# Where the value products and the side tasks stand in TensorE's attention slots

## The reference

```python
# x: (8, 512, 128); 16 heads of 8 features; everything float32
mod = (silu(c) @ wmod).reshape(8, 6, 1, 128)      # sa, ca, ga, sb, cb, gb
h = layernorm(x) * (1 + ca) + sa
q, k, v = split(h @ w_qkv)                         # to heads (8, 16, 512, 8)
attn = softmax(q @ k.T / sqrt(128))
x = x + ga * (merge(attn @ v) @ w_out)
h = layernorm(x) * (1 + cb) + sb
scores = softmax(h @ w_router)                     # 8 experts, the top 2, renormalised
y = sum_e comb[:, e] * ((silu(h @ w_gate[e]) * (h @ w_up[e])) @ w_down[e])
x = x + gb * y
```

## Time and profile before

| | us |
|---|---|
| median of 3 runs | 687.15 |
| span of the profiled execution | 679.4 |
| what lies around it, against the median | 7.75 |
| PE busy | 618.9 (91%) |
| DVE busy | 550.1 (81%) |
| ACT busy | 450.5 (66%) |
| POOL busy | 267.2 (39%) |

### The profile page before, as it was taken

How to read it: one execution, slowest core, us unless ns; L and a number is a source line. 1 busy time by engine, 2 the same in 40 slices (tenths; PEclk the granted TensorE clock), 3 DMA queues, 4 the chain that set the end, 5 groups by cost and what they waited for, 6 DMA issues and landing times.

```text
span 679.4 us, 13009 instructions
## 1 busy us (share of the span) xinstructions
PE 618.9 (91%) x3413; PEld 285.7 (42%) x3413; DVE 550.1 (81%) x1065; ACT 450.5 (66%) x859; POOL 267.2 (39%) x384
## 2 busy tenths in 40 slices
PE   5299999999999999999999999889899999999995
PEld 3112223323323322322322322225667777777773
DVE  3698889899888988988988988714788888888885
ACT  2107878778778778778778777876554555555553
POOL 4522022222222222222122122333567776776773
PEclk9658999999999999999999999979899999999999
DMA  7703505304304304303403400253334454345411
GB/s 183 197 31 82 183 3 117 106 20 106 117 19 95 126 17 95 127 17 79 143 18 72 150 18 4 76 167 109 92 114 139 137 142 141 130 137 150 136 35 31
DMA packets 48972, 65.58 MB, mean 97 GB/s; under 512 B 9432, under 2 KB 30432, under 8 KB 48928
## 3 DMA queue, kind: packets, MB, share of 16 engines
q1 hardware_dynamic: 46304, 64.32, 33.1%
q10 hardware_dynamic: 2624, 0.79, 0.5%
HBM read 47.26 MB, written 17.83 MB: 96 GB/s over the span
## 4 chain that ended last, share of the span: by engine, by line
PE 34%; DVE 20%; issue 19%; POOL 16%; ACT 5%; DMA 2%; SPq 1%; DVEq 1%; POOLq 0%; ACTq 0%
POOL hid_lo L612 13%; DVE negmax L864 13%; PE o_acc L1172 11%; PE s_row L1149 10%; PE s_col L1162 5%; ACT probs L656 3%; DVE probs L1042 1%; POOL h_lo L618 1%; PE misc L1130 1%; PE misc L1103 1%; PE misc L1100 1%; SPq L325 1%; DVE sums_inv L883 1%; DVE k_rest L878 1%; PE misc L1126 1%
## 5 line engine op out<-in xcount | busy, mean ns | idle before, releaser
L864 DVE TENSOR_REDUCE negmax<-s_row 128x1 f32<-128x512 f32 x512 | 323.0, 683 | 47.5 <-PE s_row L1149 41.9
L656 ACT ACTIVATE probs<-s_col 128x512 f32<-128x512 f32 x512 | 270.8, 599 | 76.4 <-PE s_col L1162 73.4
L1149 PE MATMUL s_row<-k_stack,q_stack 64*128 64x512 bf16 x512 | 141.7, 402 | 25.2 <-DMA k_stack<-k_scr 11.6
L612 POOL TENSOR_TENSOR hid_lo<-probs,hid_hi 128x512 fp32r<-128x512 f32 x87 | 128.5, 1493 | 61.9 <-ACT hid_hi L800 61.9
L1162 PE MATMUL s_col<-q_stack,k_stack 64*128 64x512 bf16 x512 | 132.4, 383 | 7.1 <-ACT probs L656 6.5
L1172 PE MATMUL o_acc<-probs,v_aug 128*32 128x512 f32 x1024 | 138.1, 612 | 0.0
L800 ACT ACTIVATE hid_hi<-probs 128x512 fp32r<-128x512 f32 x88 | 55.6, 632 | 85.0 <-DVE probs L1042 84.6
L1149 PEld LDWEIGHTS s_row<-k_stack,q_stack 64*128 64x128 bf16 x512 | 34.9, 93 | 180.1 <-DVE negmax L864 142.1
L1042 DVE TENSOR_TENSOR probs<-probs,q_stack 128x512 f32<-128x512 f32 x56 | 62.5, 1116 | 15.7 <-POOL hid_lo L612 13.6
L520 POOL CAST negmax_parts<-negmax 128x16 bf16<-128x16 f32 x32 | 6.3, 196 | 163.0 <-DVE negmax L864 163.0
L1032 DVE TENSOR_TENSOR probs<-probs,s_col 128x512 f32<-128x512 f32 x88 | 59.6, 677 | 2.9 <-ACT probs L820 1.6
(11 more groups left out here) (134 smaller groups left out, 713.9 us busy)
## 6 DMA issues: line engine op xcount, KB each, us to landing
q_scr<-q_parts SPq DMA_DIRECT2D x48, 128.0 KB, 2.4
k_scr<-k_parts SPq DMA_DIRECT2D x48, 128.0 KB, 2.4
q_stack<-q_scr SPq DMA_DIRECT2D x8, 768.0 KB, 6.1
k_stack<-k_scr SPq DMA_DIRECT2D x8, 768.0 KB, 7.5
q_stack<-combT_scr SPq DMA_DIRECT2D x24, 256.0 KB, 3.4
k_stack<-combT_scr SPq DMA_DIRECT2D x16, 224.0 KB, 2.9
q_stack<-combT_scr SPq DMA_DIRECT2D x16, 192.0 KB, 2.7
q_stack<-combT_scr SPq DMA_DIRECT2D x16, 160.0 KB, 2.6
```

Of the source, the lines that this page charges most:

```text
L612: nc.gpsimd.tensor_tensor(hid_lo[k % HIDDEN][:], weighed[(par + k) % 2], hid_hi[k % HIDDEN][:], ALU.subtract).then_inc(s["hid_split"], 1)
L656: nc.scalar.activation(probs[t % 2][:, j, :], s_col[score_bank("col", u)][:], ACT.Exp, scale=INV_SCALE).then_inc(s["exp_done"], 1)
L864: nc.vector.tensor_reduce(negmax[n % 2][:, j, qc:qc + 1], s_row[score_bank("row", u)][:], AX.X, ALU.max, negate=True).then_inc(s["row_max" ...
L1149: nc.tensor.matmul(s_row[score_bank("row", u)][:], q_stack[par][at:at + KS, head // 2, P * qc:P * (qc + 1)], k_stack[par][at:at + KS, head ...
```

## The change

The order on PE in a slot becomes R0 R1 C0 C1, R2 R3, W, C2 C3, task, task. No task stands at place 0 any more: both remaining places are at the end of the slot. The table TASKS is written anew for it, and with it the places at which ACT makes the middle parts of q and k, and DVE the remainders of q and k, the layer norm's statistics (two per place) and the router's steps. No instruction is added or taken away. The changed file has 20 lines less at its head, so line numbers are lower by 20.

```diff
     TASKS = {
-        (0, 0): "xT", (0, 2): "max1", (1, 0): "q", (2, 0): "k", (3, 0): "o0", (3, 2): "o1", (4, 0): "o2", (4, 2): "max2",
-        (5, 0): "o3", (5, 1): "attnT", (6, 0): "proj", (8, 1): "max3", (9, 0): "v", (10, 2): "x1T", (11, 1): "router",
-        (12, 1): "max0", (15, 0): "combT",
+        (0, 1): "xT", (0, 2): "max1", (1, 2): "q", (2, 2): "k", (3, 1): "o0", (3, 2): "o1", (4, 1): "o2", (4, 2): "max2",
+        (5, 1): "o3", (6, 1): "attnT", (7, 1): "proj", (8, 2): "max3", (9, 2): "v", (10, 2): "x1T", (11, 2): "router",
+        (12, 1): "max0", (15, 2): "combT",
     }
...
-            MIDDLE_Q, MIDDLE_K, ROUTER_EXP, FIRST_BLOCK = (2, 0), (3, 0), (12, 0), (14, 1)
+            MIDDLE_Q, MIDDLE_K, ROUTER_EXP, FIRST_BLOCK = (2, 1), (3, 1), (12, 1), (14, 1)
...
-            REST = {(1, 2): "q", (2, 2): "k"}
-            LN2_STATS = [(6, 1), (7, 0), (7, 1), (8, 0), (8, 1)]
-            ROUTE = {(12, 1): softmax_sum, (13, 0): sort, (13, 1): pick, (14, 0): denominator}
+            REST = {(2, 0): "q", (3, 0): "k"}
+            LN2_STATS = {(8, 0): (0, 1), (8, 1): (2, 3), (9, 0): (4,)}
+            ROUTE = {(12, 2): softmax_sum, (13, 1): sort, (14, 0): pick, (14, 1): denominator}
...
                 for t in range(SLOTS):
-                    def scores(j):
-                        if t < SLOTS - AHEAD:
-                            row_scores(b, par, t + AHEAD, j)
-                        elif not last:
-                            row_scores(b + 1, 1 - par, t + AHEAD - SLOTS, j)
                     for half in range(2):
                         for j in range(2 * half, 2 * half + 2):
-                            scores(j)
+                            if t < SLOTS - AHEAD:
+                                row_scores(b, par, t + AHEAD, j)
+                            elif not last:
+                                row_scores(b + 1, 1 - par, t + AHEAD - SLOTS, j)
+                        if half == 1 and t > 0:
+                            weigh(b, par, t - 1)
+                        elif half == 1 and not first:
+                            weigh(b - 1, 1 - par, SLOTS - 1)
+                        for j in range(2 * half, 2 * half + 2):
                             col_scores(b, par, t, j)
-                        turn((t, half))
-                    if t > 0:
-                        weigh(b, par, t - 1)
-                    elif not first:
-                        weigh(b - 1, 1 - par, SLOTS - 1)
+                    turn((t, 1))
                     turn((t, 2))
```

More of the change, by code:

```diff
@@ L993, in body @@
                         if not first:
-                            if at in LN2_STATS:
-                                ln2_stats(b - 1, LN2_STATS.index(at))
+                            for step in LN2_STATS.get(at, ()):
+                                ln2_stats(b - 1, step)
                             if at in ROUTE:
```

## The result

The changed kernel takes 785.35 us, the median of four runs (783.63 to 787.21), against 687.21 (686.04 to 687.64, four runs) for the kernel before beside it: 1.145 times as long (95% interval 1.140 to 1.151). Slower, as forecast, but by 98 us and not by 53. In experiments 2, 4 and 6 one of the four runs was in a slower state of the chip: it counts in the median and in the span of times given there, and not in the ratio.

The account below looks back on a forecast made before the run. PE's chain, with PE and DVE waiting for each other, was taken as the bound. Span 679.4 + 49 (six batches) + 1.5 (batch 0) + 2 (batch 7) = 732, plus 7.75 around it: 740 us; range 706 to 760.

Parts of the forecast that it names:

- The order on PE without a task: PE's slot without a task: the new order takes 2.72 us against 2.71, so the order alone is worth nothing.
- The tasks on the chain: All tasks stand between C3 and R0, uncovered on PE's chain: their products add 11.7 us a batch.
- The second task's wait: End of slots 0, 3, 4: max1 waits 1.3 us for ACT, o1 and max2 0.7 each for DVE.
- The failed step: SP's transfers for next q and k start some 4 us later, slot 8 some 6 us later: costs nothing.
- If that cover is gone, R0 of slot 8 waits a few us a batch: Proviso on SP's loads of the next q and k: uncovered, slot 8's first row product waits a few us a batch.
- The clock: Rival: PE's standstill in slot 0 halves its clock, 3 us a batch, +25, about 765 us; chance 0.10.
- ACT's and DVE's side work: ACT's moved middle parts of q and k cost nothing; DVE's extra work before maxima an estimated 1.4 us a batch.
- Batch 0: First batch, without output tasks: about 49.5 us against 47.79, +1.5.
- Batch 7: Last batch: +4 in slots 0 to 7, -2 from slot 8; together +2, give or take 4.
- What lies around the span: Time outside the profiled span: 7.75 us between span and median, taken as unchanged and added to 732.
- DVE became the bound: Rival: maxima never wait, so DVE sets the batch at 46.0 us; 651 us, weaker form 660; chance 0.10.
- Tasks bare: Rival: tasks uncovered on PE but the waits of max1 and o1 hidden, 700 to 728 us; chance 0.18.

Follow-up runs that it names:

- experiment 2: Changed kernel with the old order on PE, its task tables kept as changed: 745.84 us, ratio 1.089 to the kernel before.
- experiment 4: Changed kernel with DVE's sum of the router's exponents moved from the end of slot 12 to the middle of slot 13: 783.74 us, ratio 1.143.
- experiment 6: Changed kernel in which SP waits for max2's store before loading the next batch's q and k: 759.27 us, ratio 1.108.
- experiment 1: Kernel before with only the new order on PE, all its tasks where they were: 711.30 us, ratio 1.040.
- experiment 3: Changed kernel with ACT's placing of max2 at the head of slot 7 instead of slot 6: 765.42 us, ratio 1.117.
- experiment 5: Experiment 3 with max1, o1 and max2 moved to place 0 of the slot that follows: 732.33 us, ratio 1.066.
- experiment 9: Experiment 6 with five extra copies of the coming R0 on PE between xT and max1 in slot 0: 759.28 us, ratio 1.110.
- experiment 8: Kernel before, old PE order, with attnT, x1T, router moved to place 0, proj to slot 7, and max2's placing to slot 7: 672.03 us, ratio 0.982.

## Why the forecast held in sign and not in size

**The order on PE without a task: right.** 2.72 was worked out, 2.70 measured, with C1 at 0.85 (0.84) and no wait of the value products. That this makes the order worth nothing holds without a task only (experiment 1).

**The tasks on the chain: right.** Slots 2, 5, 8 to 12, 14 and 15, each with one task or none, came out within 0.1. DVE's wait for row products rose to 82.3 where "70 or more" was forecast, but that sign was met by luck: without the late store it is 67.0 (experiment 3) and 65.6 (experiment 6), just under it.

**The second task's wait: right.** max1 1.44 (1.3), o1 0.68 and max2 0.87 (0.7 each). Experiment 5 takes them away, and the slots become as short as slots with one task. Slot 4 is 4.65 and not 4.3: 0.2 of it is max2's longer wait, and 0.2 comes from slot 3, whose second task DVE reads out in front of slot 4's first maximum, so that R3 starts 1.34 after R0 and not 1.18 (459.77 and 461.11 in batch 6).

**The failed step: "SP's stores and loads for the next batch's q and k start some 4 us later in the batch, but slot 8, which needs them, comes some 6 us later too: nothing."** It asked only whether the loads land in time for those who read them. They do. But the transfers changed order: counted from R0 of slot 0, the first load of batch 6 moved from 17.0 to 22.0 us and max2's store from 17.1 to 23.4, so that four loads are issued just before it where one was. The store's landing goes from 4.2 us at most to 6.9, and the placing in ACT's queue waits for it with the exponents behind it. That is +2.4 in slot 6 (experiments 3 and 6: 5.78 to 3.57 by either end), and with the clock that falls behind it 25 to 27 us of the six batches (402.86 to 377.67 and 375.78), the largest part of what the forecast missed. "If that cover is gone, R0 of slot 8 waits a few us a batch" came near the size (4.2 in slots 6 and 7) by luck: it named another reader and another transfer.

On this the Trainium skill says, in "DMA: Bandwidth & Descriptors", Queues, rings and completion order, that each DMA engine takes turns between the queues that have work for it, a packet at a time. By that rule one would expect a small store on ACT's queue to pass between the packets of SP's loads and hardly be late. The trace shows otherwise: 12 KB landed after 6.9 us instead of 1.4, at 471.85, between the 768 KB of q (issued at 464.31, landed at 470.66) and the 768 KB of k (issued at 464.79, landed at 472.54). Its 64 packets aren't slow in themselves, 9 or 18 ns each, but none of them moves before 469.15, 4.2 us after the issue; from the issue up to there the 16 engines are 93% busy with packets of the loads' queue alone. In experiment 6, with no load ahead, the same packets start 0.8 us after the issue. What holds the first of them back isn't shown by a run here.

**The clock: a rival that came in addition.** It was given 0.10 and 3 us a batch. Measured are about 1.8 in slot 7 and, in half of the batches, 1.3 to 2.0 in slot 1. The prediction had put its cause in slot 0's stand of 1.3 us, and half of the batches had that stand without a fall. In slot 7 it was 1.5 to 2.4 us of standing still that came first, a consequence of the failed step. In slot 1 the cause isn't shown: the stands in slot 0 and in slot 1 lie around the falls together, and experiment 9, which fills the first, has falls still. Rival and forecast were kept apart, as if one had to be chosen; the waits that the forecast itself adds are stands of PE, and each of the nine falls in batches 1 to 6 came during a stand of 1 us or more or at most 2.3 us behind it.

**ACT's and DVE's side work: half right.** The 1.4 a batch was an estimate for DVE's steps before a maximum. Slots 8, 9, 14 and 15, where they stand, fit. Slot 13 doesn't (+1.0): the sum was moved before the first maximum of slot 13 and its exponent on ACT was moved behind two exponents of slot 12. Each move alone was looked at, and their meeting wasn't; experiment 4 takes 0.65 of it away, and 0.3 stands in batch 0 too, where no router runs.

**Batch 0**: +6.5, not +1.5. Its slots 0 and 1 had the same waits, and the clock was at one half until 63.9 where before it rose at 56.9. **Batch 7**: +3.9, +2 forecast, near it with both parts off: slots 0 to 6 took 3.0 more (+4 for slots 0 to 7 was forecast), and from slot 7 on it was +0.9, not -2, with 10.2 us at half clock in the batch where there were 6.8.

**What lies around the span**: 3.2 (785.35 against 782.2), not 7.75. In the profiled run of the changed kernel itself 1.8 lie around (784.03 against 782.2); with 1.8 around it the span before, 679.4, makes 681, below all the timed runs that stood beside it (686.04 and more). So most of the 7.75 was the difference between two executions. So the forecast of 732 for the span was short by 50, and that of 740 for the time by 45: this term took 5 off the miss, by luck.

Added up for the six batches: forecast 49, slot 6 14.6, slot 7 10.7, slot 13 5.9, slot 1 5.2, slots 0, 3 and 4 4.3: together 89.7 against 91.1 measured, the rest being rounding of the forecast row.

The other rivals fell. DVE became the bound nowhere (275.70 and 276.12 busy in a longer time). "Tasks bare" fell with the measured waits.

## What to carry to other kernels

Where steps move by different amounts, write down the order in which all queues issue their transfers, before and after: a 12 KB store behind four loads landed 5.5 us later here, and the one who waited wasn't a reader of the loads. If a bank holds the next product back on one engine, that gap is where side work costs least (slot 6 is 2.70 with attnT in the gap, experiment 8, and 3.57 with it at the end, experiments 3 and 6); an order that takes the gap away takes the cover of everything that stood in it. Placing later, so that nobody waits for the slow store (experiments 3 and 8), moves the question to the next transfer: in batch 0 the placing itself was then behind the loads. A new standstill of TensorE has two prices, the wait itself and, when the granted clock falls behind it, the slot that comes next.

## What the runs showed of the hardware

- A 12 KB store that lands after 1.4 us in the median took 6.9 and 7.8 us with 2 MB of loads issued within the 1.5 us before it, and 3.3 at most with the loads behind it (max2's store, experiment 6). Its packets start 4.2 us after the issue in the first case and 0.8 in the last.
- In the six batches the granted clock fell to one half for 3.4 or 6.8 us at a time. It fell behind the stand of slot 6 (1.5 to 2.4 us) in all six, 0.2 to 2.3 us after its end; around the two stands of slots 0 and 1 (1.3 to 1.5 and 0.9 to 1.1 us) in three batches of six, with the same instructions. No run shows which stand sets off a fall, or what else it takes.
- A product that waits holds back those behind it for the other half of the array as well: R2, whose bank had been free for some 0.6 us, started 0.01 us behind C1 (80.02 and 80.03). Without a wait R0 and R1 start together although C0 stands between them.
